# Expert results stored as a dense table and gathered by token, with the last shared work behind the tiles

## What is computed

```python
def _L0_ffn_ref(x, sW1, sb1, sW2, sb2, rW1, rb1, rW2, rb2, gW, gb):
    shared_enc = _expert_stack(x, sW1, sb1, sW2, sb2).sum(0)
    weights = jax.nn.softmax(x @ gW + gb, axis=-1)
    topv, topi = jax.lax.top_k(weights, TOP_K)
    gated = (jax.nn.one_hot(topi, E_ROUTER, dtype=weights.dtype) * topv[..., None]).sum(axis=-2)
    router_out = _expert_stack(x, rW1, rb1, rW2, rb2)
    router_enc = jnp.einsum('ebtd,bte->btd', router_out, gated)
    return shared_enc + router_enc + x
...
x = _layernorm(x + _L0_ffn_ref(x, ...), axis=-1)
```

## Time and profile before

| | us |
|---|---|
| median of 3 timed runs (lowest, highest) | 285.84 (283.21, 287.46) |
| span of the profiled execution | 319.6 |
| of it up to the first copy of a tile | 209.16 |
| the 62 tiles, to the end of the last product | 102.44 |
| from there to the end | 8.0 |

### The profile page before, as it was taken

One profiled execution on the slowest core, in us unless ns is written; L12 is line 12 of the kernel. 1 busy time (PEld: TensorE's weight loads), 2 busy tenths in 40 slices (PEclk: granted clock), 3 DMA queues, 4 the chain that ended last, 5 costly groups with the idle time before them and its releaser, 6 DMA issues.

```text
span 319.6 us, 7117 instructions
## 1 busy us (share of the span) xinstructions
PE 241.1 (75%) x2283; PEld 179.8 (56%) x2283; DVE 221.6 (69%) x630; ACT 192.2 (60%) x423; POOL 179.0 (56%) x166
## 2 busy tenths in 40 slices
PE   6989989877988767996761299688868867785970
PEld 3676868655535434452451156586857757674960
DVE  6777999989999998998520497043444434856875
ACT  4697997549976976754470350344554546563665
POOL 6132755330666738985677467135656566665752
PEclk9999999999997998998978589799999999999778
DMA  7672830124000002952211133123132263354462
GB/s 218 217 213 46 181 128 2 37 67 133 2 0 2 0 4 62 378 215 49 86 58 50 44 101 108 41 61 101 53 99 76 75 187 90 91 168 123 150 185 90
DMA packets 38597, 31.89 MB, mean 100 GB/s; under 512 B 12864, under 2 KB 31552, under 8 KB 38432
## 3 DMA queue, kind: packets, MB, share of 16 engines
q1 hardware_dynamic: 34608, 23.90, 26.6%
q0 software_dynamic: 3520, 7.27, 6.7%
q10 hardware_dynamic: 432, 0.27, 0.3%
HBM read 19.95 MB, written 11.47 MB: 98 GB/s over the span
## 4 chain that ended last, share of the span: by engine, by line
PE 44%; DVE 27%; issue 14%; ACT 4%; another core or an unknown queue 4%; POOL 4%; DMA 1%; DVEq 0%; SPq 0%; ACTq 0%
PE psum L994 12%; PE psum L985 9%; PE psum L783 5%; DVE prob_sums L1496 4%; PE psum L763 4%; DVE maxes L1490 3%; PE psum L977 2%; PE psum L568 2%; DVE prob_sums L1410 2%; POOL x_srt L1986 2%; PE psum L585 1%; DMA xT<-x_t 1%; DVE turned_room L1421 1%; DVE maxes L1405 1%
## 5 line engine op out<-in xcount | busy, mean ns | idle before, releaser
L2047 POOL DMA_INDIRECT y_tok<-k_heads,y_rows x62 | 62.7, 1012 | 50.8 <-ACT k_heads L1327 34.4
L1319 ACT ACTIVATE k_heads<-psum,k_heads 128x128 f32<-128x128 f32 x124 | 38.7, 365 | 38.5 <-PE psum L985 33.6
L1986 POOL DMA_INDIRECT x_srt<-v_blocks,slot x48 | 48.0, 1000 | 21.3 <-issue 17.2
L994 PE MATMUL psum<-k_heads 128*128 128x128 f32 x248 | 42.4, 295 | 18.0 <-issue 12.1
L1823 DVE COPY k_heads<-psum 128x128 f32<-128x128 f32 x62 | 17.8, 289 | 48.9 <-PE psum L977 32.7
L994 PEld LDWEIGHTS psum<-k_heads 128*128 128x128 f32 x248 | 34.2, 200 | 21.9 <-issue 15.2
L985 PE MATMUL psum<-k_heads 128*128 128x128 f32 x248 | 40.6, 288 | 5.2 <-DVE k_heads L1823 4.2
L1963 POOL TENSOR_TENSOR k_heads<-k_heads,inv_sums 128x1024 f32<-128x1024 f32 x14 | 27.1, 1939 | 24.0 <-DVE inv_sums L1503 23.9
L985 PEld LDWEIGHTS psum<-k_heads 128*128 128x128 f32 x248 | 33.8, 198 | 8.5 <-DVE k_heads L1823 7.4
L1951 POOL TENSOR_TENSOR probs<-probs,inv_sums 128x512 f32<-128x512 f32 x16 | 16.8, 1050 | 28.9 <-DVE inv_sums L1415 28.7
L1327 ACT ACTIVATE k_heads<-psum,k_heads 128x128 f32<-128x128 f32 x62 | 22.9, 370 | 11.3 <-PE psum L994 9.1
(11 more groups left out here) (191 smaller groups left out, 530.1 us busy)
## 6 DMA issues: line engine op xcount, KB each, us to landing
expert_w<-e_w SPq DMA_DIRECT2D x1, 4369.0 KB
k_heads<-x_srt SPq DMA_DIRECT2D x62, 65.0 KB
q_heads<-y_tok SPq DMA_DIRECT2D x8, 256.0 KB
x_srt<-pad SPq DMA_DIRECT2D x16, 65.0 KB
xT<-x_t SPq DMA_DIRECT2D x4, 256.0 KB, 5.1
ctxT_k<-ctx_k SPq DMA_DIRECT2D x2, 512.0 KB, 5.5
v_scr<-v_rows SPq DMA_DIRECT2D x4, 256.0 KB, 2.8
ctxT_v<-ctx_v SPq DMA_DIRECT2D x2, 512.0 KB, 5.0
```

Source lines behind the costliest of these rows:

```text
L994: mm = pe.matmul(bank[6 + t % 2][:, 0:E], h_tile[:, t % 2, a, :], tile_weights(t)[:, FE + E * a:FE + E * a + E], start=(a == 0), stop=(a = ...
L1319: ins = act.activation(h_tile[:, t % 2, a, :], bank[2 + t % 2][:, P * a:P * a + P], ACT.Gelu, bias=tile_weights(t)[:, EW - 2 + a:EW - 1 + a])
L1986: pool.indirect_dma_start(out=x_srt, out_offset=bass.IndirectOffsetOnAxis(ap=slot[:, n:n + 1], axis=0), in_=payloads[:, g, k, :], in_offse ...
L2047: pool.indirect_dma_start(out=y_tok, out_offset=bass.IndirectOffsetOnAxis(ap=y_rows[:, t:t + 1].bitcast(mybir.dt.uint32), axis=0), in_=y_t ...
```

## The change

The results of the tiles go to a dense table `y_srt` in the order of the tiles, two tiles with one transfer of SyncE (`y_stored`). They are not scaled by gates and not scattered. For each chunk GpSimd gathers the three results of each group with 12 indirect DMAs (`gathered`, 48 in all) as soon as the tiles that hold them are stored; for chunk 0 in two halves, for chunk 3 with a semaphore for each group and, for the last group, for each choice. VectorE works out where a pair's row lies in `y_srt` (`y_map_...`, `y_slots`), with single instructions spread over tiles 0 to 41, and multiplies by the gate when it adds (`added`, `last_added`). Payloads go: a row of `x_srt` is the token alone, all three choices are scattered from `x2`, and a scatter no longer waits for gates and copies. SyncE loads tile t+8 when tile t is turned, and reads the late count once for four tiles, up to tile 15 (LATE). `shared_in` of chunk 3 and `shared_out` of chunks 2 and 3 stand behind the tiles, and so do the sums of chunk 2 and all roots. The last chunk is finished in two parts, three groups and then the last group of 128 tokens.

The diff, cut to what matters here:

```diff
 SOON = (NC - 1) * 4 * TOPK
 NB = 8
+NY = 4
 NS = 5
-XW = E + 2
-ROWS = NE * ROOM + P
+LATE = 4
...
-    x_srt = nc.dram_tensor("x_srt", [ROWS, XW], F32).ap()
-    y_tok = nc.dram_tensor("y_tok", [NT * P + TOPK * T, E], F32).ap()
+    x_srt = nc.dram_tensor("x_srt", [NE * ROOM + P, E], F32).ap()
+    y_srt = nc.dram_tensor("y_srt", [NT * P, E], I32).ap()
...
-        RELOAD_LAG = 9
-        RELOAD_LAST = 57
-        SUMS_AT = (39, 48, 57)
-        ROOTS_AT = 52
-        SHARED_TILES = (8, 14, 20, 26)
+        SUMS_AT = (47, 57)
+        Y_SLOTS_AT = (1, 16, 25, 34)
...
+            def x_loaded(t, rows):
+                if t < 4 * LATE:
+                    if t % 4 == 0:
+                        sp.wait_ge(s_late_rows, late_at)
+                elif t == 4 * LATE:
+                    sp.wait_ge(s_late_rows, late_rows)
+                sp.dma_start(x_tile[:, t % NB, :], x_srt[bass.ds(rows[t % 4], P), :]).then_inc(s_x_tile[t % NB], 16)
+
+            def y_stored(p):
+                sp.wait_ge(s_y_tile, 2 * p + 2)
+                if p >= NY:
+                    sp.wait_ge(s_y_stored[p % NY], 16 * (p // NY))
+                sp.dma_start(y_srt[2 * P * p:2 * P * p + 2 * P, :].rearrange("(a p) e -> p a e", p=P),
+                             y_tile[:, 2 * p % NB:2 * p % NB + 2, :].bitcast(I32)).then_inc(s_y_stored[p % NY], 16)
+
+            late_at = rows_of(0)
             sp.wait_ge(s_tables, 1)
+            x_rows_at = x_row_of(0)
             sp.wait_ge(s_filled, 16 * (NE + 1))
             sp.wait_ge(s_scattered, 16 * (SOON - 1))
+            for t in range(NB):
+                if t == 4:
+                    late_at = rows_of(1)
+                    x_rows_at = x_row_of(4)
+                x_loaded(t, x_rows_at)
             for t in range(NT):
...
+                if t + NB < NT:
...
+                    sp.wait_ge(s_tile_turned, t + 1)
+                    x_loaded(t + NB, x_rows_at)
+                if t % 2 == 1:
+                    y_stored(t // 2)
+            for g in range(NG - 1):
                 sp.wait_ge(s_final, g + 1)
-                store(sp, 1, g)
...
+                store(sp, g // 4, g % 4)
+            sp.wait_ge(s_final_v, 1)
+            store(sp, NC - 1, 3)
...
             gates_turned(1)
-            shared_in(6)
-            shared_in(7)
-            shared_out(2, 0)
-            shared_out(2, 1)
-            shared_out(2, 2)
-            shared_out(2, 3)
...
-                if i in SHARED_TILES:
-                    shared_out(NC - 1, SHARED_TILES.index(i))
+            shared_in_late(0)
+            shared_in_late(1)
+            shared_out(2, 0)
...
+            shared_in_late(2)
+            shared_in_late(3)
+            shared_out(3, 0)
...
-            def payload(c):
-
-                act.wait_ge(s_x2, 4 * c + 4)
-                for k in range(1, TOPK):
-                    act.copy(payloads[:, 4 * c:4 * c + 4, k, 0:E], x2[:, 4 * c:4 * c + 4, :]).then_inc(s_payloads, 1)
-
...
                     if t >= NB:
-                        act.wait_ge(s_y_scattered[t % NB], 16 * (t // NB))
-                    act.activation(y_tile[:, t % NB, :], bank[6 + t % 2][:, 0:E], ACT.Copy,
-                                   scale=x_tile[:, t % NB, E:E + 1]).then_inc(s_y_tile, 1)
+                        act.wait_ge(s_y_stored[t // 2 % NY], 16 * (t // 2 // NY))
+                    act.copy(y_tile[:, t % NB, :], bank[6 + t % 2][:, 0:E]).then_inc(s_y_tile, 1)
...
+            def y_slots(c, n):
+                cols = slice(12 * c, 12 * c + 12)
+                if n == 0:
+                    routed(dve.tensor_tensor(mapped, one_hot[:, c, :, :].unsqueeze(2).broadcast_to([P, 12, 3, NE]),
+                                             y_map[:, c, :, :].unsqueeze(1).broadcast_to([P, 12, 3, NE]), ALU.mult))
+                elif n == 2:
+                    routed(dve.tensor_reduce(moved, mapped, AX_X, ALU.add))
+                elif n == 4:
...
+                elif n == 7:
+                    dve.tensor_tensor(y_slot[:, cols], slot[:, cols], moved[:, :, 0], ALU.subtract).then_inc(s_y_slots, 1)
 
             def added(c, k):
-                if c < NC - 1:
-                    dve.wait_ge(s_y_loaded[c], 16 * TOPK)
-                else:
-                    dve.wait_ge(s_y_last[k], 16)
                 if k == 0:
+                    dve.wait_ge(s_y_got[c], 16 * 4 * TOPK)
                     dve.wait_ge(s_acc, c + 1)
+                    dve.wait_ge(s_gates, NC)
                 else:
                     dve.wait_ge(s_y_sum, 4 * c + k)
-                dve.tensor_tensor(acc[:, 4 * c:4 * c + 4, :], acc[:, 4 * c:4 * c + 4, :],
-                                  routed_y[k][:, 4 * c:4 * c + 4, :], ALU.add).then_inc(s_y_sum, 1)
+                for g in range(4 * c, 4 * c + 4):
+                    ins = dve.scalar_tensor_tensor(out=acc[:, g, :], in0=routed_y[k][:, g, :], scalar=gate_cols[:, g, k:k + 1],
+                                                   in1=acc[:, g, :], op0=ALU.mult, op1=ALU.add)
+                ins.then_inc(s_y_sum, 1)
...
+            root_seed(0, NC - 2)
+            for n in range(3):
+                root_newton(0, NC - 2)
+            sum_mean(0, NC - 2)
+            shared_result(2)
+            for k in range(TOPK):
+                added(NC - 2, k)
+            sum_stats(NC - 2)
+            shared_result(NC - 1)
             root_seed(NC - 2, NC - 1)
...
+            for j in range(3):
+                dve.wait_ge(s_y_last[j], 16 * TOPK)
+                for k in range(TOPK):
+                    last_added(NG - 4 + j, k)
+                last_stats(NG - 4 + j)
+            last_root(NG - 4, NG - 1, 1)
+            for k in range(TOPK):
+                dve.wait_ge(s_y_end[k], 16)
+                last_added(NG - 1, k)
+            last_stats(NG - 1)
+            last_root(NG - 1, NG, 2)
...
                     if n % 12 == 0:
                         pool.wait_ge(s_slots, g // 4 + 1)
-                        pool.wait_ge(s_payload_gates, g // 4 + 1)
-                        pool.wait_ge(s_payloads, 2 * (g // 4) + 2)
+                        pool.wait_ge(s_x2, g + 4)
...
-            for t in range(NT):
-                pool.wait_ge(s_y_tile, t + 1)
-                pool.wait_ge(s_y_rows, t // 4 + 1)
-                pool.indirect_dma_start(out=y_tok, out_offset=bass.IndirectOffsetOnAxis(
-                    ap=y_rows[:, t:t + 1].bitcast(mybir.dt.uint32), axis=0),
-                    in_=y_tile[:, t % NB, :], in_offset=None).then_inc(s_y_scattered[t % NB], 16)
+            pool.wait_ge(s_landed, 1)
...
+            def gathered(n):
...
+                pool.indirect_dma_start(out=routed_y[k][:, g, :].bitcast(I32), out_offset=None, in_=y_srt,
+                                        in_offset=bass.IndirectOffsetOnAxis(ap=y_slot[:, n:n + 1], axis=0)).then_inc(got, 16)
+
+            def tiles_through(counts):
+                for k in range(NY):
+                    pool.wait_ge(s_y_stored[k], counts[k])
+                pool.sem_inc(s_y_through, 1)
+
+            half, first = landed(0), landed(1)
+            tiles_through(half)
+            pool.wait_ge(s_y_slots, 1)
+            for n in range(2 * TOPK):
+                gathered(n)
+            tiles_through(first)
+            for n in range(2 * TOPK, 4 * TOPK):
+                gathered(n)
+            for c in range(1, NC):
+                counts = landed(c + 1)
+                tiles_through(counts)
+                pool.wait_ge(s_y_slots, c + 1)
+                for n in range(4 * TOPK * c, 4 * TOPK * (c + 1)):
+                    gathered(n)
```

343 lines of the change are left out of this document (183 added, 160 removed).

## The result

The changed kernel took 289.60 us in the median of 4 runs (288.18 to 291.23), the kernel before 286.65 (4 runs, 283.21 to 288.31). The ratio is 1.016, 95% interval 1.008 to 1.024: slower by 1.6%, where -0.2% was forecast. The ratios here compare the fast executions of both kernels alone, so they are not the quotients of the medians.

What follows compares the result with a forecast made beforehand. No engine is full in the tile loop; tiles wait for each other, 32 us taken as waiting. -2.0 - 6.1 - 5.0 - 13.4 + 25.9 = -0.6 us of 319.6, so 285.3 us on the timed median, range 271 to 298.

Steps and rivals of the forecast that it cites:

- the term -13.4 of the loop: Tile loop: 32 us of waiting belongs to 62 scatters, 36 gathers bring back 18.6, so -13.4 us.
- Front, -2.0: Before the tiles: payload copies go and scatters no longer wait for gates, -2.0 us, bounds 0 and -4.
- Start, -6.1: Start of the tiles: the first tile copy moves from 209.16 to 203.0 us, -6.1, bounds 0 and -7.
- loop without shared work, -5.0: Tile loop: the last quarter of shared work leaves it, -5.0 us.
- The end, 28.65 us plus 5.2 for delayed hand-overs: Last tile's product to the end: 13.8 us TensorE, 14.85 VectorE, ten hand-over delays; 33.9 against 8.0, +25.9 us.
- Gathers: GpSimd's 48 gathers at 1.26 us each end about when VectorE reaches the last group, costing nothing there.
- the forecast's -0.6: Whole kernel: all terms sum to -0.6 us of 319.6, or -0.2%; chance 0.30.
- Rival C: Whole kernel: timed runs have none of these waits; 83.7 us behind the first copy becomes 85.9; 288 us, chance 0.12.
- Rival A: Tile loop: waits come from what scatters are coupled to, so it runs at 1.03 us per tile; 274 us, chance 0.30.
- Rival B: Tile loop: TensorE's late hand-overs stay, 1.57 us per tile, only the end counts; 294 us, chance 0.26.
- The slow gathers: Behind the loop: fp32 copies block GpSimd's descriptors, 24 last gathers take 82 us, kernel 50 us longer; chance 0.02.

Runs made afterwards that it cites:

- k1: The kernel before, unchanged, profiled a second time: span 284.4 us.
- k9: The kernel before with the loop's 62 scatters replaced by plain stores on GpSimd's queue: 0.984 times the kernel before.
- k4: The changed kernel with gathers reading the experts' weights, so that they wait for no tile: 1.016 times the kernel before.
- k6: The changed kernel with shared work of chunks 2 and 3 placed as before, earlier sums and roots of chunks 0 and 1: 1.017 times the kernel before.
- k12: The changed kernel with 56 tiles in place of 62 and sums of chunks 0 and 1 from tiles 46 and 52: 0.989 times the kernel before.
- k15: The kernel before with 56 tiles in place of 62, last reload at tile 55, chunk 2's sum behind the loop: 0.991 times the kernel before.
- k5: The changed kernel with shared work of chunks 2 and 3 placed as before and gathers waiting for no tile: 1.015 times the kernel before.
- k8: The changed kernel with chunk 2's shared work before the tiles, chunk 3's behind tiles 55 to 58, earlier sums and roots: 1.000 times the kernel before.
- k11: The changed kernel with late shared work before tile 57 and sums, roots and stores of chunks 0 and 1 earlier: 1.025 times the kernel before.
- k3: The changed kernel with shared work of chunk 2 back before the tiles and of chunk 3 back inside the loop: 1.010 times the kernel before.
- k17: The changed kernel with shared work, sums and roots moved earlier and the last chunk's four groups finished together: 1.004 times the kernel before.

## Why the prediction was wrong

The step that failed is the term -13.4 of the loop, and it failed before any edit was priced. "The rest, 102.4 - 65.3 - 5.0 = 32 us, is waiting" and "If the 32 us of waiting belong to the 62 scatters, 0.52 each" took late hand-overs of one execution as a property of the loop, and the timed median, 33.8 us below the profiled span, was only carried along. In k1 the same remainder is 84.4 - 65.3 - 5.0 = 14.1 us, and in the changed kernel 72.9 - 65.3 = 7.6 (187.82 to 260.72): the change brings back 6.5, not 13.4. The text said that it was a coincidence seen in one trace and still built its largest gain on it. What is left in k1 has in part another cause, GpSimd's unbroken queue at 1.30 us per scatter, worth 4.2 us by k9; the other 9.9 us stay open.

Against the terms of the sum, counted on after and k1:

- Front, -2.0: measured -2.0 in the means of fourteen and four profiles. The size is right; that it is so to a tenth is luck, since it was taken between bounds of 0 and -4 and single executions spread over 5 us.
- Start, -6.1, loop without shared work, -5.0, and fewer waits, -13.4, together -24.5: measured -15.4 (from the 48th scatter to the end of the last tile product 62.4 us, in k1 77.8). Of that the first copy has -3.9, counted like the rest (187.82 against 191.20 from the start), in place of -6.1: in the clean profile it was not that late to begin with. The loop has -11.5 (84.4 to 72.9), in place of -18.4.
- The end, 28.65 us plus 5.2 for delayed hand-overs, against 8.0: measured 28.8 against 8.8, so +20.0. The 28.65 came out to 0.2 us, but by errors that cancel: TensorE took 13.3 us, not 13.8; the three groups of chunk 3 took 5.1 (277.15 to 282.27), not 2.5 + 1.35, since their nine additions took 1.16 us per group and not 0.83; the last store took 2.5, not 3.1. The 5.2 came from the same false frame.
- Gathers: 1.26 us each assumed, 1.29 found (0.99 and 0.30). They were to end "about when VectorE comes to the last group"; they end at 275.25, 8.3 us before that (283.59), so that they cost nothing there, as it said. The 14 us that GpSimd idles before the first follow from "the first six gathers go after tile 15", but were not priced; k4 shows that they cost the changed kernel about 1 us or nothing.
- The net: -15.4 + 20.0 = +4.6 behind the scatters, -2.0 before them, +2.6 us; timed +1.6% (0.8 to 2.4), some 4 us. The difference is inside the spread of the executions. Against the forecast's -0.6 the loop and its start were 9.1 us too hopeful and the end 5.9 too dark. Both errors came from the false frame and in part cancelled; that the total missed by so little is luck.

Rival C had the right frame ("the timed runs have none of these waits") and gave 288, +2.2 us, at 0.12. Its two lengths behind the first copy, 83.7 and 94.0 us, were 93.2 and 101.7: before the change it had the scatters begin 3.2 us after the first copy, where they begin at 6.9 (198.11 against 191.20), the row scatters being ahead of them, at 1.26 in place of 1.30, and 12.5 us from the 54th to the end, where k1 has 16.3; after the change its end was right and its loop 7.6 us short. These errors too nearly cancel. Rival A (274) is out: the loop did fall to 1.0 us per tile between the sums, but so does k1's between its stops, and the gain was less than the end cost. Rival B had the sign of the result. Its own sign was a gain of less than 0.12 us per tile in the loop, and k1 against the changed kernel is just that: (84.4 - 5.0 - 72.9)/62 = 0.10. But its mechanism, late hand-overs that stay, is in none of the profiles of 280 to 290 us. The slow gathers (0.02) are out: the gathers run beside the same 128x514 copies at 978 to 1008 ns. The Trainium skill (SBUF — State Buffer, SBUF: two separate sides) would have GpSimd unable to write descriptors beside such copies; no slowing of that size shows. Single gathers of 1.28 us stand beside VectorE's sums in k6 (1.28 at 250.06, the sums 1.13 each), a third longer and not three times.

Nowhere did the prediction say that the changed sums are longer. It counted them in the 28.65, so this did not make its sum wrong; but against an end of 8.0 us that in the kernel before holds only the last chunk, it could not show where the change loses. From the same piece of work on, the sum of chunk 2, it does: 16.4 against 21.8.

## What to carry to other kernels

When the profiled execution is longer than the timed runs by more than their spread, its extra waits are not the kernel's: take a second profile, and look for queues that have no gaps, before pricing waits. A queue without gaps need not be worth its whole length either: here 4 us came back with it (k9). Work moved behind a loop of fixed length pays for the iterations that the data leave empty, on every engine that runs them in order (six empty tiles: 8 us after the move, k12, 3 us before it, k15). And when taking away the chain that seems to end last gives nothing (k4, k5), look for a stretch of constant length, here VectorE's tail of 20 us, and then only for what starts it.

## What the runs showed of the hardware

An indirect DMA costs GpSimd 0.95 to 1.0 us and 0.30 until the next, scattering or gathering, from a table just written or from the weights (k4: means of 953 and 1009 ns in its two groups); a plain store of the same 64 KB on the same queue 0.55 us (k9). Single ones take longer: a gather up to 1.42 us (k8, at 218.34), a scatter of tokens up to 2.00 (k11, at 136.84).

TensorE's granted clock differs between executions of nearly the same instructions. The stretch 150 to 190 us (stretch, length, busy time and count of TensorE, its loads, VectorE, ScalarE and GpSimd, clock, DMA share, GB/s), of k3 and of k6:

```profile
150.00:190.00 40.00, 33.81 (x224) 24.61 (x224) 26.74 (x112) 19.48 (x39) 30.06 (x31) 1.00 0.32 100
```

```profile
150.00:190.00 40.00, 36.64 (x209) 26.80 (x208) 25.25 (x109) 17.76 (x34) 29.75 (x31) 0.83 0.29 89
```

k3 ran it at the upper level, 2.4 GHz; k6, with 0.83 in the mean, partly at 1.2, and its TensorE was busy longer for fewer matmuls. In the 150 us before both ran at a mean of 0.98, TensorE 123 us busy. What made the grant differ, no run here shows. Nor does this pair show what it costs a whole execution: k6 reached the end of its 48th scatter 2.1 us before k3. Over the 97 timed runs of the kernel before that stand beside k1 to k17 (281.87 to 290.26 us, the one of 414.05 left out) those with the higher mean clock tend to be the shorter ones (correlation -0.63), which is no proof of a cause.
